# A causal mask moved from a TensorE matmul into the seeds of the diagonal score tiles, with the jobs of the queues in another order

## What is computed

```python
k = jnp.einsum('ihd,bpd->biph', W_K, x); q = jnp.einsum('ihd,bpd->biph', W_Q, x)
v = jnp.einsum('ihd,bpd->biph', W_V, x)
scores = jnp.einsum('biph,biqh->biqp', k, q)
mask = jnp.tril(jnp.ones((pos, pos)))
masked = scores * mask - 1e10 * (1.0 - mask)
attn = softmax(masked / sqrt(d_head)); z = jnp.einsum('biqp,biph->biqh', attn, v)
out = jnp.einsum('df,bqf->bqd', W_O, z_flat)
# then: x + out * silu(ffn(xn))
```

## Time and profile before

| | |
|---|---|
| time, median of 3 runs | 1405.44 us (1404.18 to 1406.34) |
| the profiled execution | 1405.89 us |
| its span, first to last instruction | 1404.1 us |
| PE busy | 1377.4 us (98%) |
| DVE busy | 1214.9 us (87%) |
| ACT busy | 1090.0 us (78%) |
| POOL busy | 865.8 us (62%) |

### The profile page before, as it was taken

How to read it: one execution, slowest core, us unless ns; L and a number is a source line. 1 busy time by engine, 2 the same in 40 slices (tenths; PEclk the granted TensorE clock), 3 DMA queues, 4 the chain that set the end, 5 groups by cost and what they waited for, 6 DMA issues and landing times.

```text
span 1404.1 us, 23095 instructions
## 1 busy us (share of the span) xinstructions
PE 1377.4 (98%) x7596; PEld 1166.5 (83%) x7596; DVE 1214.9 (87%) x2636; ACT 1090.0 (78%) x2267; POOL 865.8 (62%) x705
## 2 busy tenths in 40 slices
PE   5999999999999999999999999999999999999997
PEld 4887888888888888888888888888888888887886
DVE  6789898799898988889888898889888898888977
ACT  2687886888778787788877888688877888777675
POOL 5555774656666575666755676466656757576456
PEclk9999999999999999999999999999999999999999
DMA  3100001010110101100010000101010000010003
GB/s 97 31 16 16 16 9 46 8 22 10 31 23 9 24 9 30 31 16 8 16 38 16 16 16 12 43 9 24 8 31 24 16 16 16 16 35 16 24 9 105
DMA packets 30134, 33.73 MB, mean 24 GB/s; under 512 B 11072, under 2 KB 17728, under 8 KB 30016
## 3 DMA queue, kind: packets, MB, share of 16 engines
q1 hardware_dynamic: 30016, 32.26, 9.6%
HBM read 30.02 MB, written 2.23 MB: 23 GB/s over the span
## 4 chain that ended last, share of the span: by engine, by line
PE 93%; DVE 4%; ACT 1%; issue 1%; DMA 0%; DVEq 0%
PE ps L319 27%; PE ps L321 27%; PE ps L320 27%; PE ps L817 9%; PE ps L877 2%; PE ps L829 1%; DVE p_lo L640 1%; DVE partmax L687 1%; DVE stats L605 0%; DMA acc<-x_dram 0%; DVE acc L633 0%; DVE acc L729 0%; DVE xT_lo L681 0%; ACT p_hi L582 0%; DVE kT_lo L681 0%
## 5 line engine op out<-in xcount | busy, mean ns | idle before, releaser
L498 POOL TENSOR_TENSOR colsum<-colsum,probs 128x512 f32<-128x512 f32 (+3 forms) x512 | 657.8, 1285 | 244.4 <-ACT probs L581 208.4
L640 DVE TENSOR_TENSOR p_lo<-probs,p_hi 128x512 fp32r<-128x512 f32 (+3 forms) x640 | 532.9, 839 | 17.6 <-ACT p_hi L582 17.3
L581 ACT ACTIVATE probs<-ps 128x512 f32<-128x512 f32 (+3 forms) x640 | 344.5, 538 | 170.1 <-PE ps L321 99.6
L552 ACT ACTIVATE ps<-maxrow 128x512 f32<-128x512 f32 (+3 forms) x640 | 355.3, 555 | 0.1
L582 ACT ACTIVATE p_hi<-ps 128x512 fp32r<-128x512 f32 (+3 forms) x640 | 344.5, 538 | 0.0
L687 DVE TENSOR_REDUCE partmax<-ps 128x1 f32<-128x512 f32 x384 | 256.3, 680 | 4.7 <-PE ps L817 2.7
L319 PE MATMUL ps<-p_hi,v_hi 128*128 128x512 f32 (+3 forms) x640 | 240.1, 375 | 2.4 <-DVE p_lo L640 2.2
L319 PE MATMUL ps<-qT_hi,kT_hi 128*128 128x512 f32 (+3 forms) x640 | 236.0, 369 | 1.1 <-ACT ps L552 1.0
L817 PE MATMUL ps<-kT_hi,qT_hi 128*128 128x512 f32 (+3 forms) x640 | 231.4, 383 | 4.2 <-DVE partmax L693 1.7
L321 PE MATMUL ps<-p_hi,v_lo 128*128 128x512 f32 (+3 forms) x640 | 233.1, 364 | 0.0
L320 PE MATMUL ps<-qT_lo,kT_hi 128*128 128x512 f32 (+3 forms) x640 | 233.1, 364 | 0.0
(11 more groups left out here) (119 smaller groups left out, 2294.1 us busy)
## 6 DMA issues: line engine op xcount, KB each, us to landing
spread<-max_dram SPq DMA_DIRECT2D x64, 256.0 KB, 4.0
wraw<-wqk_dram SPq DMA_DIRECT2D x16, 256.0 KB, 4.3
acc<-x_dram SPq DMA_DIRECT2D x4, 512.0 KB, 6.8
wraw<-wv_dram SPq DMA_DIRECT2D x8, 256.0 KB, 4.9
wraw<-wo_dram SPq DMA_DIRECT2D x8, 256.0 KB, 3.7
out_dram<-acc SPq DMA_DIRECT2D x8, 256.0 KB, 2.1
max_dram<-rowmax SPq DMA_DIRECT2D x64, 2.0 KB, 1.4
maxrow<-x_dram SPq DMA_DIRECT2D x2, 512.0 KB, 3.9
```

Source lines behind the costliest of these rows:

```text
L498: nc.gpsimd.tensor_tensor(total[:, c0:], total[:, c0:], tile[:, c0:], ALU.add)\
L552: nc.scalar.activation(st[job.n % SCORE_BANKS][:, c0:], maxrow[:, job.g, c0:], ACT.Copy)\
L581: nc.scalar.activation(probs[:, k, c0:], src, ACT.Exp, scale=SCALE).then_inc(probs_ready, 1)
L640: nc.vector.tensor_tensor(p_lo[:, k, c0:], probs[:, k, c0:], f32(p_hi[:, k, c0:]), ALU.subtract)\
```

## The change

The bf16 matmul on the diagonal tiles, its two constants and their four set-up instructions on GpSimd are gone. In their place GpSimd makes, once for each of the 64 query blocks, a second row of maxima with -1e10 where a key comes after the query (one `affine_select` of 128 x 512, `mask_maxima`), into two halves of the buffer `gates[:, 1]`, which was idle until the feed-forward; the gates of two blocks there trade places (`gate`). The seed of a diagonal tile becomes two ScalarE instructions, the first 128 columns from the masked row and the others from the plain one; on the fourth diagonal tile, which has 128 columns, it stays one. All four order strings are new. The core of the diff:

```diff
-        ident_bf = sb("ident_bf", [P, P], BF16)
-        mask_bf = sb("mask_bf", [P, P], BF16)
+        masked = gates[:, 1].rearrange("p t d -> p (t d)").rearrange("p (k n) -> p k n", k=2)
+MASK_AHEAD = 6
+        for block, gi in enumerate(max_blocks):
+            head, g = divmod(gi, NB)
+            diagonal = first_tile[gi] + TB * g
+            mask_at.append(max(order_at[block], diagonal - MASK_AHEAD))
...
+            def mask_maxima(block):
+                pool.wait_ge(max_ordered, block + 1)
+                if block >= 2:
+                    pool.wait_ge(seeded, tiles_until(max_blocks[block - 2]))
+                nc.gpsimd.affine_select(out=masked[:, block % 2, :].rearrange("p (t n) -> p t n", t=TB),
+                                        in_=maxrow[:, max_blocks[block] % NB, :].rearrange("p (t n) -> p t n", t=TB),
+                                        compare_op=ALU.is_ge, fill=MASKED, base=0, pattern=[[0, TB], [1, P]],
+                                        channel_multiplier=-1).then_inc(max_masked, 1)
...
+                while masks < len(max_blocks) and mask_at[masks] <= n:
+                    mask_maxima(masks)
+                    masks += 1
                 total, tile = colsum[:, gi % 2, :], probs[:, n % PROBS, :]
                 pool.wait_ge(probs_ready, n + 1)
...
-                c0 = columns(job)
-                nc.scalar.activation(st[job.n % SCORE_BANKS][:, c0:], maxrow[:, job.g, c0:], ACT.Copy)\
-                  .then_inc(seeded, 1)
+                dst, c0, plain = st[job.n % SCORE_BANKS], columns(job), columns(job)
+                if job.kt // TB == job.g:
+                    block = max_blocks.index(job.head * NB + job.g)
+                    plain = c0 + P
+                    act.wait_ge(max_masked, block + 1)
+                    op = nc.scalar.activation(dst[:, c0:plain], masked[:, block % 2, c0:plain], ACT.Copy)
+                if plain < BW:
+                    op = nc.scalar.activation(dst[:, plain:], maxrow[:, job.g, plain:], ACT.Copy)
+                op.then_inc(seeded, 1)
...
-                    if job.kt // TB == job.g:
-                        op = nc.tensor.matmul(dst[:, 0:P], ident_bf[:, :], mask_bf[:, :], start=False, stop=True,
-                                              skip_group_check=True)
                     op.then_inc(scores_ready, 1)
...
 START = (
-    "m0 n0 m1 n1 N00 N10 m2 Pq00 n2 Pk00 N01 N11 M0010 M0000 M0020 M0030 Pq01 Pk01 M0110 N02 m3 n3 M0111 M0120 "
-    "V01 M0100 M0130 M0101 M0131 "
+    "m0 n0 m1 n1 N00 N10 m2 Pk00 N01 Pq00 N11 M0020 M0000 M0010 M0030 n2 Pq01 m3 M0110 n3 N02 V01 Pk01 M0130 "
+    "M0111 M0100 M0101 M0120 M0131 "
 )
```

More of the change, by code:

```diff
@@ L26 @@
 F32R = mybir.dt.float32r
-BF16 = mybir.dt.bfloat16
 P = 128
@@ L272, in attention_layer @@
         max_ordered = sem("max_ordered")
+        max_masked = sem("max_masked")
         bits_set = sem("bits_set")
@@ L307, in attention_layer @@
                 order_at.append(tile and min(tile - 1 + ORDER_LAG, first_tile[job.head * NB + job.g] - SEED_AHEAD))
+        mask_at = []
+        for block, gi in enumerate(max_blocks):
+            head, g = divmod(gi, NB)
+            diagonal = first_tile[gi] + TB * g
+            mask_at.append(max(order_at[block], diagonal - MASK_AHEAD))
+        assert mask_at == sorted(mask_at) and max_blocks == sorted(max_blocks)
         def columns(t):
@@ L329, in gate @@
         def gate(b):
-            return (gates[:, 0], token_rows(wraw[:, 0:2, :]), gates[:, 1], token_rows(spread[:, :, :]))[b]
+            return (gates[:, 0], token_rows(wraw[:, 0:2, :]), token_rows(spread[:, :, :]), gates[:, 1])[b]
         def gated_rows(b):
@@ L443, in _ @@
             nc.gpsimd.memset(ident[:, :], 0.0).then_inc(made, 1)
-            nc.gpsimd.memset(ident_bf[:, :], 0.0).then_inc(made, 1)
-            nc.gpsimd.memset(mask_bf[:, :], 0.0).then_inc(made, 1)
             nc.gpsimd.memset(mask_rows[:, :], 0.0).then_inc(made, 1)
@@ L450, in _ @@
                 nc.gpsimd.memset(rank[:, :, e:e + 1], float(E - e))
-            pool.wait_ge(made, 5)
+            pool.wait_ge(made, 3)
             diagonal = dict(compare_op=ALU.not_equal, base=0, pattern=[[-1, P]], channel_multiplier=1)
             nc.gpsimd.affine_select(out=ident[:, :], in_=ident[:, :], fill=1.0, **diagonal)
-            nc.gpsimd.affine_select(out=ident_bf[:, :], in_=ident_bf[:, :], fill=1.0, **diagonal)
-            nc.gpsimd.affine_select(out=mask_bf[:, :], in_=mask_bf[:, :], compare_op=ALU.is_ge, fill=MASKED,
-                                    base=0, pattern=[[1, P]], channel_multiplier=-1)
             nc.gpsimd.affine_select(out=mask_rows[:, BW - P:], in_=mask_rows[:, BW - P:], compare_op=ALU.is_ge,
@@ L463, in _ @@
             split_weights(wraw[:, 1, :], flat(wv_hi[:, :, :]), flat(wv_lo[:, :, :]), wv_in, 16, 2, wv_ready)
-            his, finals = 2, 0
+            def mask_maxima(block):
[6 more added lines that the diff above has]
+                                        channel_multiplier=-1).then_inc(max_masked, 1)
+            his, masks = 2, 0
+            finals = 0
             for job in plan:
@@ L738, in _ @@
                         dve.wait_ge(ffn_w_ready, DC)
+                    if job.b == 2:
+                        dve.wait_ge(max_ordered, len(max_blocks))
                     if job.b == 3:
-                        dve.wait_ge(max_ordered, len(max_blocks))
+                        dve.wait_ge(seeded, PAIRS * TILES)
                     nc.vector.tensor_tensor(
```

## The result

The changed kernel takes 1389.66 us (median of 4 runs, 1387.54 to 1390.37) against 1405.89 for the kernel before in the same job: a ratio of 0.9885, interval 0.9874 to 0.9897. The gain is 16.2 us; the prediction gave 28.8 and a range that ended at 1385.0. The profiled execution takes 1389.27 us, 1.9 us above its span of 1387.4.

A forecast was written before the change was run, and what follows sets the result against it. TensorE bounds the kernel, busy 1377.4 of 1404.1 us. Span 1404.1 - 31.4 (masks) + 2.0 (start) + 0.6 (new waits) = 1375.3; + 1.8 - 0.45 to the median gives 1376.6 us, range 1370 to 1385.

The forecast's parts named there:

- What a mask costs: On TensorE, each of 256 mask matmuls adds 0.1225 us, all on the path: removing them gains 31.4 us.
- The estimate of 20.7 us by the Trainium skill: On TensorE, 256 masks at the skill's 0.081 us each; the prediction used the trace's 0.123 us instead.
- Seeds and selects cost nothing themselves: Split seeds on ScalarE (at most 35 us) and 64 GpSimd selects (39 to 99 us) stay off the path: cost nothing.
- VectorE held up by selects: On VectorE, selects lengthen `p_lo` by 39 to 99 us, to at most 1314 us in 1373: not a bound.
- 16 us to spare: VectorE's slack in a middle pair, its share going from 87.7% to 89.9%.
- 0.1 us of new waits a pair: In the middle pairs, an allowance on top of 162.1 us each for VectorE's higher share; 0.6 us in all.
- The bound of 6 us: Upper bound on the new waits in all middle pairs, taken as 0.6 us; lower bound 0.
- The rival of new waits: VectorE held up by selects, or split seeds late: 2 us a pair, 1393 us, down to 1383; chance 0.09.
- The start: The new order delays the first score from 36.31 to 39 to 40.5 us: +2 us, bounds -1 and +5.5.
- First and last pair: In the first and last pairs of heads the prediction saw no reason for either sign.

The follow-up runs named there:

- the kernel without contention: The changed kernel with GpSimd's column sums cut to their last column, every instruction, wait and place kept: 1372.77 us, ratio 0.9765.

## Why the prediction was wrong

**What a mask costs: right.** 0.1225 us forecast; 0.128 in the kernel without contention, where a pair's 32 masks bring 4.1 us. The estimate of 20.7 us by the Trainium skill ("TensorE: Matmul & The Clock Gate", "Back-to-back issue gap") would have been 2.6 us a pair; the measurement decides.

**Seeds and selects cost nothing themselves: right in size.** A select took 803 ns at the mean, 0.9 forecast:

```profile
L472 POOL TENSOR_SCALAR_AFFINE_SELECT gates<-maxrow 128x512 f32<-128x512 f32 x64 | 51.4, 803 | 24.6 <-ACT maxrow L557 24.6
```

In the middle pairs ScalarE never waits for a select. TensorE's weight loads wait for seeds there, 4.6 us in all six, which they did not before; the kernel without contention has the same waits (4.7 us) and takes 161.9 us a pair, so they cost nothing that shows.

**VectorE held up by selects, "tight in places, not a bound": the step that failed.** The amount looks right, 39.4 us more against 39 to 99, and is so by chance. Selects account for little of it (4.9 us more `p_lo` on the old order, 2 us behind running selects on the new); the new order alone, without one, lengthens `p_lo` as much as the whole change. I priced the added instruction and never the shift of the old ones. And I set the sum over a pair, 16 us to spare, against a wait that arises in a few microseconds at the pair's end, where VectorE has hardly a gap and a late `p_lo` makes the next one late. The kernel before had that already, in the last ten tiles of a pair (columns as in the earlier trace rows):

```profile
523.50:540.90 17.40, 17.40 (x91) 14.50 (x91) 17.25 (x34) 15.09 (x33) 14.70 (x11) 1.00 0.09 16
```

VectorE is busy for 17.25 of 17.40 us there, 99% and not 88%.

**"0.1 us of new waits a pair": the term that was mis-sized.** Five pairs took 2.5 to 2.7 us more than the 162.2 forecast, one 0.3, in all 13.1 us. The bound of 6 us was too near as well; from the earlier trace rows, a `p_lo` of 1809 ns beside a median of 682, one collision a pair costs up to 1.1 us before anything follows from it. The rival of new waits had the right price (2 us a pair) at a chance of 0.09, with the wrong culprits.

**The start: right by the number, not all by the reason.** The first score came at 39.80, forecast 39 to 40.5, and with the order alone at 39.60. But the old order is as late with the new seeds (39.59, behind the select), so either half alone makes the start late by as much as both. I charged the order alone, and did not see that the select would have cost the same on the old order.

**First and last pair: no sign was forecast.** The first pair went from 172.6 to 168.0 us, 0.7 us more than the masks' 3.9, and from the last pair's first score to the end it went from 199.1 to 193.3, 2 us more.

The Trainium skill, "SBUF — State Buffer", "Who interferes with whom", says that such a pair of instructions exclude each other and that the one issued first keeps the way for its whole length. The table above agrees, 679 against 1112 to 1235 ns. I used the first half against the select, and did not ask what the second half does to instructions that were there already.

**Open**: which moved job of the new order sends 31 more `p_lo` behind a running GpSimd instruction (313 against 282, without a select) was not isolated, nor why tile 70 went the other way in the fifth middle pair alone. What takes the gain back on the old order is not shown: with the new seeds (165.0 us a pair) and without masks (163.6) `p_lo` takes hardly longer than before (537.8 and 531.3 us against 532.9), so it is not new collisions. That the collisions of before, which a slower TensorE did not feel, are enough there is possible, but was not tried with the sums cut on that order.

## What to carry to other kernels

When a change takes work off an engine that was busy all the time, ask what its speed and a new order do to the phase of two other engines that share something, not only what the added instructions cost. Headroom over a stage is no cover for a wait; look for the place where the second engine has no gap, and for the spread of its durations: here a tail of 1.8 us on a median of 0.7 meant that another engine decided them. Where order of arrival decides, one wait at the right place, for an instruction about to begin, can bring much (here 10 us, beside 16 for the whole change), and the same wait everywhere can cost more than it brings.

## What the runs showed that I had not expected

- 0.27 us in the arrival of a column sum decides 2.2 us of a pair: the loser waits out the winner, and the next tiles inherit the order.
- Taking work away made the kernel slower: without its selects the changed kernel takes 6.5 us more. In each middle pair a select had kept GpSimd's next instructions from starting ahead of the `p_lo` of tiles 54 and 55.
- The change's two halves are worth nothing apart: the order alone +0.8%, the seeds alone -0.05% (no difference that can be told), together -1.15%.
